# An attention and gated feed-forward kernel on one core: moving the product of q ahead of the transpositions, and the order of small steps around it

## What is computed

```
xn = ln(x, g_norm)
q = (xn @ Wq).reshape(b, n, 16, 64).transpose(0, 2, 1, 3)
k, v = split(xn @ Wkv)                      # one head; a null key and value are put ahead
q = q / |q| * q_scale ;  k = k / |k| * k_scale
sim = einsum('bhid,bjd->bhij', q, k) * 8 + rel_pos_bias      # causal and key masks
attn = softmax(sim)
out = einsum('bhij,bjd->bhid', attn, v).transpose(...) @ Wout
y = ln(out, g_out)
xq = quantise(y) ; h = quantise(silu(xq @ Wg.T) * (xq @ Wu.T)) ; result = x + h @ Wd.T
```

## Time and profile before

| | |
|---|---|
| time, median of 3 (lowest to highest) | 299.08 us (297.76 to 299.78) |
| the profiled execution: its own time | 299.08 us |
| its span, first to last instruction | 297.3 us |
| busy share PE / DVE / ACT / POOL | 87% / 80% / 77% / 69% |
| granted TensorE clock, mean | 0.970 |

### The profile page before, as it was taken

One profiled execution on the slowest core, in us unless ns is written; L12 is line 12 of the kernel. 1 busy time (PEld: TensorE's weight loads), 2 busy tenths in 40 slices (PEclk: granted clock), 3 DMA queues, 4 the chain that ended last, 5 costly groups with the idle time before them and its releaser, 6 DMA issues.

```text
span 297.3 us, 7308 instructions
## 1 busy us (share of the span) xinstructions
PE 257.9 (87%) x2161; PEld 203.5 (68%) x2162; DVE 238.1 (80%) x969; ACT 230.0 (77%) x781; POOL 204.6 (69%) x394
## 2 busy tenths in 40 slices
PE   0769999999999999999999999999999989975270
PEld 0427777787888778877887888788878767751060
DVE  2768978798879878888888798787877788869893
ACT  1554978888898899889988988889888897259380
POOL 2277979788878887887888888788877785013300
PEclk9989999999999999999999999999999999999857
DMA  4179100000000000000000000000000020000013
GB/s 142 33 191 264 21 1 2 1 2 1 3 0 2 4 1 2 0 3 1 2 0 4 3 0 2 0 4 0 2 0 4 1 73 3 2 0 0 1 37 110
DMA packets 13084, 6.89 MB, mean 23 GB/s; under 512 B 1954, under 2 KB 12914, under 8 KB 13043
## 3 DMA queue, kind: packets, MB, share of 16 engines
q1 hardware_dynamic: 11874, 6.03, 7.7%
q10 hardware_dynamic: 1168, 0.36, 0.6%
HBM read 5.31 MB, written 1.07 MB: 21 GB/s over the span
## 4 chain that ended last, share of the span: by engine, by line
PE 60%; DVE 20%; POOL 8%; issue 5%; DMA 4%; ACT 2%; SPq 1%; POOLq 0%; DVEq 0%; ACTq 0%
PE bank L904 14%; PE front L881 7%; PE bank L855 7%; PE back L947 7%; PE bank L744 6%; POOL prob L448 6%; PE back L881 5%; PE front L947 4%; DVE score L1276 4%; DMA g1b<-in_L_cond_g_dram 4%; PE bank L760 3%; DVE oT L1266 2%; DVE hmax L1428 2%; DVE oT L1464 2%; DVE yn L1299 1%
## 5 line engine op out<-in xcount | busy, mean ns | idle before, releaser
L589 ACT ACTIVATE prob<-score,negmax 128x258 f32<-128x258 f32 (+1 forms) x256 | 113.4, 449 | 17.8 <-DVE negmax L1276 17.7
L448 POOL TENSOR_SCALAR prob<-prob,rrow 128x258 f32<-128x258 f32 x254 | 107.9, 443 | 22.0 <-DVE rrow L1284 20.1
L401 POOL TENSOR_TENSOR rq<-qn,neghalf 128x8 f32<-128x8 f32 x32 | 53.3, 1666 | 2.7
L589 ACT ACTIVATION_READ_ACCUMULATOR prob<-score,negmax 128x1 f32 x256 | 49.2, 192 | 0.0
L904 PE MATMUL bank<-pT,val 128*64 128x256 f32 x496 | 47.1, 332 | 0.0
L1276 DVE CUSTOM_DVE_ANT_0 score<-front,bias 128x258 f32<-128x258 f32 (+1 forms) x128 | 38.2, 354 | 8.0 <-PE front L881 7.8
L904 PEld LDWEIGHTS bank<-pT,val 128*64 128x64 f32 x496 | 30.8, 136 | 19.3 <-ACT pT L599 9.9
L1145 DVE TENSOR_REDUCE qn<-sq 128x8 f32<-128x512 f32 x32 | 21.9, 684 | 23.7 <-ACT sq L535 23.7
L1276 DVE CUSTOM_DVE_ANT_0 score<-back,bias 128x258 f32<-128x258 f32 (+1 forms) x128 | 38.0, 353 | 0.1
L855 PE MATMUL bank<-wout,oT 128*128 128x128 f32 x256 | 36.7, 287 | 1.2 <-DVE yn L1299 1.1
L599 ACT COPY pT<-back 128x384 f32<-128x384 f32 x62 | 28.8, 481 | 9.0 <-PE back L947 8.6
(11 more groups left out here) (203 smaller groups left out, 465.0 us busy)
## 6 DMA issues: line engine op xcount, KB each, us to landing
bias<-relative_table SPq DMA_DIRECT2D x8, 256.0 KB, 5.0
out_dram<-prob SPq DMA_DIRECT2D x4, 256.0 KB, 3.0
X<-in_x_dram SPq DMA_DIRECT2D x1, 896.0 KB, 13.9
prob<-in_L_cond_Wq_dram SPq DMA_DIRECT2D x1, 512.0 KB, 5.4
wout<-in_L_cond_Wout_dram SPq DMA_DIRECT2D x1, 512.0 KB, 15.1
prob<-in_L_ffn_w_down_dram SPq DMA_DIRECT2D x1, 176.0 KB, 2.4
X<-in_x_dram SPq DMA_DIRECT2D x1, 128.0 KB, 4.3
prob<-in_L_ffn_w_gate_dram SPq DMA_DIRECT2D x1, 128.0 KB, 2.2
```

What stands on the lines that cost most here:

```text
L401: pool.tensor_tensor(dst, src, neghalf[:, 0:width], ALU.pow).then_inc(done, 1)
L448: pool.tensor_scalar(prob[:, par, h, cols], prob[:, par, h, cols], rrow[:, par, h, t:t + 1], 1.0, ALU.mult, ALU.mult).then_inc(normed, 1)
L589: act.activation(prob[:, par, h, cols], score[:, h % 4, cols], ACT.Exp, scale=-1.0, bias=negmax[:, par, h, t:t + 1], accum_out=rowsum[:, p ...
```

## The change

Order alone is changed: no instruction is added or removed, apart from `values`' one wait, which becomes one wait for each pair of heads.

- PE: `q_make` moves from behind `turn` 3 to ahead of `turn` 0 in the same group. `values` waits for the first two copies before its first half, and for all four before its second.
- The chunk's squares (ACT), sums (DVE) and power (POOL) move from group `at`+1 into group `at`: ACT behind `exponent` 1, DVE behind the second `invert`, POOL between the two `normalise` calls. `q_normalise` moves to the start of DVE's group, ahead of `oT_copy` (at g = 2 behind it).
- ACT: the small copies (kv, k, x, y) stand ahead of `pT_evac` 2 and 3, and not behind.
- POOL: x's power stands behind q's, y's power one group earlier (g = 1), k's power in the group of kv, all three behind `normalise` of the turned heads.
- DVE: k's scaling moves from the middle of its group to the end (in sample 0 it stays in the middle); k's transposition goes to g = 2, x's to g = 1; `y_stats` stands ahead of the transposed q's copy, `y_normalise` ahead of `oT_copy`, `yT_absmax` goes to g = 3, and in group 1 `xT_split_low` goes to the start.

The diff, with context cut:

```diff
@@ -77,8 +77,9 @@
         self.kv = self.next if self.g == late else None
-        self.kT = self.next if self.g == 1 + late else None
-        self.xT = self.b + 2 if self.g == 2 + late and self.b + 2 < B else None
+        self.kz = self.next if self.g == 1 + late else None
+        self.kT = self.next if self.g == 2 else None
+        self.xT = self.b + 2 if self.g == 1 + 2 * late and self.b + 2 < B else None
         self.yT = self.prev if self.g == 3 else None
...
@@ -449,18 +450,18 @@
             def group(s):
-                if s.kT is not None:
-                    k_power(s.kT)
-                if s.g == 2 and s.prev is not None:
-                    y_power(s.prev)
-                if s.g == 3 and s.b + 3 < B:
-                    x_power(s.b + 3)
-                if s.quarter is not None and s.quarter >= 4:
-                    q_power(s.quarter, s.quarter % 4)
                 if s.turned is not None:
...
                     x_power(2)
+                if s.g == 1 and s.prev is not None:
+                    y_power(s.prev)
+                if s.made is not None:
+                    q_power(s.made, s.made % 4)
+                if s.g == 3 and s.b + 3 < B:
+                    x_power(s.b + 3)
+                if s.kv is not None:
+                    k_power(s.kv)
                 normalise(heads(s.at)[0:2])
...
@@ -469,7 +470,6 @@
-                y_power(B - 2)
                 normalise(heads(LOOP - 1)[2:4])
...
@@ -609,8 +609,6 @@
             def group(s):
-                if s.quarter is not None and s.quarter >= 4:
-                    q_square(s.quarter, q_ps)
                 if s.turned is not None:
...
@@ -620,22 +618,24 @@
                 exponent(heads(s.at)[1])
+                if s.made is not None:
+                    q_square(s.made, q_ps)
                 if s.turned is not None:
...
                     kv_evac(s.kv, front_tails)
-                if s.turned is not None:
-                    pT_evac(s.turned, 2)
-                    pT_evac(s.turned, 3)
-                if s.null is not None:
-                    null_evac(s.null)
                 if s.kT is not None:
...
                     yT_evac(s.yT)
+                if s.turned is not None:
+                    pT_evac(s.turned, 2)
+                    pT_evac(s.turned, 3)
+                if s.null is not None:
+                    null_evac(s.null)
                 if s.first and s.g == 1:
...
@@ -887,10 +887,6 @@
                 m, g = at // GB, at % GB
-                if at == LOOP:
-                    pe.wait_ge(pTe_ready, GH)
-                else:
-                    pe.wait_ge(pT_ready, GH * (at if at > LOOP else at + 1))
                 if g == 0:
...
@@ -899,6 +895,10 @@
                 for pair in range(2):
+                    if at == LOOP:
+                        pe.wait_ge(pTe_ready, 2 * pair + 2)
+                    else:
+                        pe.wait_ge(pT_ready, GH * (at - 1 if at > LOOP else at) + 2 * pair + 2)
                     for blk, c0, c1, i0 in ((1, 0, N, 0), (0, N, N + P, P)):
...
@@ -1029,6 +1029,12 @@
                     y_null(s.prev)
+                if s.made is not None:
+                    if s.made % 4 == 0:
+                        if s.first:
+                            pe.wait_ge(wq_low, 1)
+                        pe.wait_ge(xT_low, s.next)
+                    q_make(s.made, s.made % 4, s.made // 4 % 2, q_ps)
                 if s.turned is not None:
...
@@ -1037,12 +1043,7 @@
                     turn(s, 3)
-                if s.made is not None:
-                    if s.made % 4 == 0:
-                        if s.first:
-                            pe.wait_ge(wq_low, 1)
-                        pe.wait_ge(xT_low, s.next)
-                    q_make(s.made, s.made % 4, s.made // 4 % 2, q_ps)
+
             def over_partitions(k):
...
@@ -1321,30 +1322,34 @@
             def group(s):
-                if s.quarter >= 4:
-                    q_norm2(s.quarter, s.quarter % 4)
-                if s.summed is not None:
-                    oT_copy(s.summed)
                 if s.g == 2 and s.prev is not None:
                     y_normalise(s.prev)
+                    oT_copy(s.summed)
+                if s.quarter >= 4:
+                    q_normalise(s.quarter, s.quarter % 4, q_ps)
+                if s.summed is not None and not (s.g == 2 and s.prev is not None):
+                    oT_copy(s.summed)
+                if s.at == 1:
+                    xT_split_low(1, 1)
                 if s.first:
...
                     invert(heads(s.turned)[2:4])
-                if s.kT is not None:
-                    k_normalise(s.kT)
-                if s.quarter >= 4:
-                    q_normalise(s.quarter, s.quarter % 4, q_ps)
+                if s.kz is not None and s.first:
+                    k_normalise(s.kz)
                 score_pair(heads(s.at)[2:4])
...
                 invert(heads(s.at)[0:2])
+                if s.g == 1 and s.prev is not None:
+                    y_stats(s.prev)
+                if s.made is not None:
+                    q_norm2(s.made, s.made % 4)
                 if s.quarter > 2:
...
                 if s.at == 1:
-                    xT_split_low(1, 1)
                     x_stats(2)
...
@@ -1352,11 +1357,11 @@
                     k_norm2(s.kv)
+                if s.kz is not None and not s.first:
+                    k_normalise(s.kz)
                 if s.g == 0 and s.prev is not None and s.b + 2 < B:
                     x_normalise(s.b + 2)
-                if s.g == 1 and s.prev is not None:
-                    y_stats(s.prev)
-                if s.g == 2 and s.b > 1:
+                if s.g == 3 and s.b > 1:
                     yT_absmax(s.b - 2)
...
@@ -1373,8 +1378,8 @@
                 score_pair(heads(LOOP)[2:4])
+                y_normalise(B - 2)
                 oT_copy(LOOP - 2)
-                y_normalise(B - 2)
                 invert(heads(LOOP)[0:2])
...
```

## The result

The changed kernel takes 295.96 us (median of 4 runs, 295.09 to 296.73) against 298.94 (4 runs, 297.76 to 299.78): a ratio of 0.989, with a 95% interval from 0.986 to 0.992, so about 1% faster. I had said 294.2, range 291.2 to 297.7, and faster. The profiled execution took 295.77 with a span of 293.9, so 3.4 us of span are gone. The lines of DVE and POOL have moved by one: scores L1277, `q_normalise` L1152, `oT_copy` L1267, the power L402.

What follows compares the result with a forecast made beforehand. PE's work and its waits bound the kernel, with q's loop the expected new limit. Sample 0 -2.1, sample 1 -0.8, steady samples -2.2, groups 28 and 29 -0.1, ending +0.35: 299.1 - 4.9 = 294.2 us, range 291.2 to 297.7.

Steps and rivals of the forecast that it cites:

- The new limit: Steady groups: q's chain becomes a loop from scores to scores of 7.00 us, against PE's 6.72 at g = 2 and 3.
- The rival that the loop is hidden: Steady samples: the loop counts for 6.7 and all 0.99 us of stalls go, near 291 us; chance 12%.
- the rival of a loop of 7.2: Steady samples: a longer loop stalls PE 1.06 us a sample, no steady gain, 297.3 us; chance 20%.
- What makes up the stalls: Steady samples: PE stalls 0.27 us at g = 3 and 0.28 at g = 0 for oT_copy, 0.55 a sample against 0.99.
- a sign that I had listed myself as one of being wrong: Steady groups: PE waiting inside values for ACT would show the forecast wrong; no size given.
- the one on the small copies: ACT's copies: the fourth ends at 7.33 (g = 2) and 7.87 (g = 1), needed at 7.44 and 7.89; costs nothing.
- The second rival: k's scaling on DVE waits out POOL's q power, costing 1.0 us a sample more than now, about 303 us; chance 6%.
- Sample 0: Pipeline fill: PE's stalls of 0.54 and 0.64 us go, group 4 starts at 51.2 against 53.24: a gain of 2.1.
- group 2 starts at 36.7: Sample 0: walking groups 1 to 3 by the same durations puts group 2's start at 36.7 and group 3's at 43.7.
- Samples 1 to 6: Sample 1 falls from 29.06 to 28.25 us, -0.8; five steady samples at -0.44 each, -2.2.
- Groups 28 and 29: Last groups ahead of the ending, with no small products and, in 29, no q product: -0.1 us.
- The ending: Pads cleared and weights about 1.5 us later against group 30's start, less DVE's 1.11 standing still: a loss of 0.35.

Runs made afterwards that it cites:

- the kernel with the added operation: The changed kernel with one more small POOL operation ahead of the clamp in q's power, its result unread: 301.08 us (1.007).
- the second experiment: The changed kernel with ACT's pT copies of heads 2 and 3 ahead of the small copies again: 296.4 us (0.991).
- the first three: The changed kernel with oT_copy ahead of q_normalise in all groups; with pT copies ahead of the small ones; with both: 293.2, 296.4 and 292.59 us.
- the last three: Both orders mended, plus kv's copy first in group 1; then q_normalise ahead of oT_copy in group 2; then y_normalise before group 30's scores: 290.83, 291.48, 291.5 us.
- The last experiment: y_normalise of sample 6 ahead of group 30's first scores, on the kernel with q_normalise ahead of oT_copy in group 2: 291.5 us (0.973).

## Why the prediction was right, and where it wasn't

*The new limit.* Right in place and size: a loop of 6.96 us (7.00), sample 28.30 (28.25), PE no longer waiting for POOL, DVE waiting for it in three groups of four. The size is no luck of the sum, for the parts fit one by one: 0.46, 1.78, 1.49 and 2.03 from the scores at 133.65 to `q_normalise` at 139.41, and 1.20 from `q_normalise` at 132.45 to those scores, for the predicted 0.47, 1.77, 1.55, 2.03 and 1.18. Lengthening the loop by 0.2 showed it by experiment. The rival that the loop is hidden is refuted with it; the rival of a loop of 7.2 is nearly what the kernel with the added operation ran as: it priced a sample at 27.70 + 1.06 = 28.76, and at 7.15 the run took 28.97.

*What makes up the stalls.* Wrong in composition, and by a sign that I had listed myself as one of being wrong, PE waiting inside `values` for ACT: I had 0.55 a sample as two waits for `oT_copy` and none in `values`. The waits are 0.14 and 0.05 for `oT_copy`, and 0.24, 0.18 and 0.05 in `values` (g = 2, 0, 3): 0.66. The step that failed is the one on the small copies, "7.87, against a need at 7.44 and 7.89. Nothing": the copies end at 124.50 - 116.60 = 7.90 as worked out, but I took the need from the matmuls, and the weight loads want them 0.17 sooner (124.49 less 124.32). The sum came out near all the same, 0.66 for 0.55, and the second experiment says why: the loop fixes the sample, so a late copy only uses slack that the loop leaves to PE. PE also follows `oT_copy` by 0.05 and not by 0.15, which makes the waits for `oT_copy` shorter than mine.

*DVE behind POOL's power.* The second rival is refuted: no DVE operation is held by the power. DVE's and POOL's timelines where k's scaling meets q's power:

```profile
123.76 0.61 DVE L1135 SCALAR_TENSOR_TENSOR kz<-kv,rk,qks 128x128 f32<-128x128 f32 x2
```

```profile
123.85 0.34 POOL L400 TENSOR_SCALAR qn<-qn 128x8 f32<-128x8 f32 x1
124.28 1.67 POOL L402 TENSOR_TENSOR rq<-qn,neghalf 128x8 f32<-128x8 f32 x1
```

The scaling's two operations take 0.61 together, and POOL's clamp beside them 0.34 instead of 0.24. At 109.72 a DVE subtraction of two SBUF operands (x's split) runs in 0.42 wholly inside the power of 109.40 to 111.07. The rule of the Trainium skill that the prediction weighed (SBUF — State Buffer, engine ports) would have put these behind each other, whichever started second. The trace disagrees where POOL's power starts first: the subtraction of 109.72 was not held. Where DVE's operation starts first or with it, POOL's takes longer, by less than a full wait. Two powers of the changed kernel show it: one of 1.84 at 67.16, beside k's scaling of 66.87, and one of 1.94, where x's split and q's power start together:

```profile
80.81 0.41 DVE L1123 TENSOR_TENSOR xTl<-xTr,xTh 128x256 fp32r<-128x256 f32 x1
```

```profile
80.82 1.94 POOL L402 TENSOR_TENSOR rq<-qn,neghalf 128x8 f32<-128x8 f32 x1
```

The others take 1.67; the split takes its usual 0.41. The same meeting, within 0.01 us, gives 1.93 or 1.94 in six of the experiments' profiles (the first three and the last three), and the clamp's 0.34 above is of the same kind, begun 0.09 behind k's scaling. It is a test of the loop that nobody had planned: in the changed kernel the group of that power (80.65 to 88.22) takes 7.57 us where the four later ones with g = 0 take 7.28 to 7.30, and sample 2 takes 28.59; in the kernel with `oT_copy` first the same long power costs nothing (7.18, as in the later samples).

*Sample 0.* Right in sign and mechanism, too large in size: -1.34 for -2.1, inside its bounds of 1.0 to 2.8. Both old stalls went and the new one in group 3 is there with 0.84 for 0.7. The step that failed is "group 2 starts at 36.7": it started at 37.49, 0.32 of that from the later first scores and 0.33 from a wait for a pT copy that I had not walked through. The other 0.14 of it I have not traced. From there group 3 came 7.05 later (walked as 7.0) and group 4 another 7.68 (walked as 7.5); of those 0.18, 0.14 are the longer wait for `oT_copy`.

*Samples 1 to 6.* -2.46 for -3.0. Sample 1 gave 0.63 for 0.8 (29.06 before, 28.43 after), the other five 1.83 for 2.2, 0.07 a sample less than I had; some 0.3 of the shortfall is the long power in sample 2.

*Groups 28 and 29.* +0.42 for -0.1, a wrong sign: group 28 gained 0.22 (6.89 for 7.11), group 29 lost 0.64 (7.14 for 6.50). The step "with no small products and, in 29, no q product: -0.1" took them as steady groups. Without q's product in group 29 nothing pushes the transpositions back, and the fourth head's waits for POOL again. PE:

```profile
232.47 1.16 PE L855 MATMUL bank<-wout,oT 128*128 128x128 f32 x8 [0.25 <-DVE oT L1267]
...
235.00 1.14 PE L947 MATMUL back<-ident,prob 128*128 128x128 f32 x6
```

Six transpositions take 1.14 where they take 0.82 elsewhere: the wait of 0.3 that the change removed is back, with 0.25 for `oT_copy` besides.

*The ending.* -0.34 for +0.35, the other term with the wrong sign. The clearing did move, from 0.93 us behind group 30's start (240.31 less 239.38) to 2.19 (238.51 less 236.32), and the weights with it (DVE's timeline, answering to the earlier trace rows):

```profile
243.19 0.95 DVE L1238 TENSOR_REDUCE wmax<-prob 128x6 f32<-128x768 f32 x1 [1.93 <-DMA prob<-in_L_ffn_w_down_dram]
244.06 0.42 DVE L1277 CUSTOM_DVE_ANT_0 score<-front,bias 128x258 f32<-128x258 f32 x1
```

The reduction is 6.87 us behind group 30's start (236.32) instead of 5.71, so 1.2 later where I had 1.5; it ends as the scores are due, with no wait between, and 1.11 of slack held all of it. The step that failed is the size of the shift: 0.3 less, and the loss was gone. Of the gain, 0.14 lies between the first scores of groups 30 and 31 (6.53 for 6.67), where PE waits 0.94 for `oT_copy` and not 1.11 for `y_normalise`; the other 0.20, behind group 31's start, stays open. The last experiment shows how thin the slack is: what PE won ahead of group 31 went to DVE's wait for this transfer.

In sum 294.2 was 1.8 low: 0.8 from sample 0, 0.5 from samples 1 to 6, 0.5 from groups 28 and 29, 0.3 from the first 27 us, less 0.7 from the ending; that is 1.4, and the rest is rounding and the difference between one execution and a median.

## What to carry to other kernels

When a step is moved to an earlier place in a software pipeline, write down the whole circle of waits from it to itself in the next group and add it up, small hand-overs included; compare that with the bound engine's work a group: here the circle, 6.96 us against 6.72, set the time, and no engine's busy share showed it. If an instruction waits in a queue ahead of one that the bound engine needs, swap the two: here that alone gave up to 2.8 us where the whole change gave 3.0, and with ACT's copies swapped too, 0.2 us more a group on POOL cost at most 1.5 us instead of 5.1. Mend the circle first: the second wait, mended alone, showed nothing. And take the time at which PE needs an operand from its weight loads, not from its matmuls.

## What the runs showed of the hardware that I had not expected

The stretch before the first scores holds the same instructions in every kernel here (two experiments add POOL's small operation), yet the scores began at 26.93 us (before), 27.25 (after), and between 26.39 and 28.18 in the ten experiments: 1.8 us apart. The windows of 0 to 26 us, first before, then after (last three columns: granted clock, DMA share, GB/s):

```profile
0.00:26.00 26.00, 13.44 (x43) 7.45 (x44) 14.69 (x49) 11.77 (x24) 11.64 (x29) 0.93 0.53 138
```

```profile
0.00:26.00 26.00, 13.40 (x40) 7.57 (x40) 14.81 (x49) 11.19 (x23) 12.03 (x29) 0.87 0.56 141
```

The granted clock over these 26 us was 0.93 in the three profiles with the earliest first scores (26.39, 26.73 and 26.93) and 0.87 in the nine others (27.25 and later). It is an association in twelve profiles; neither the clock nor the transfers were varied on purpose. From 52 to 222 us the granted clock is 1.00 in all twelve, so the differences between steady samples are not of this kind. For this kernel it means that one profile against another can't tell apart what is under about 1 us, unless it is read from a fixed point such as the first scores.

The other is that hand-overs differ between pairs of engines: PE began 0.05 us after DVE's `oT_copy` ended (133.74 to 133.79) and DVE 0.03 after POOL's power (132.42 to 132.45), but POOL's clamp 0.18 after DVE's sums (130.24 to 130.42). The same three gaps recur wherever these pairs meet in this profile, to 0.02 us.
